# Four dense tiles from bf16 pieces in a graph kernel's counts pass, and two row buffers between its passes

## The reference

```
L0: x += ssp(segment_sum(h[dst] * filter(edge) * cutoff, src) @ W + b) @ W + b
L1: x += attention over edges, softmax by destination, values h @ W
L2: x += relu( (D_dst^-1/2 * segment_sum((D_src^-1/2 h)[src], dst)) @ W + b )
L3: two convolutions, out = segment_sum((dinv h)[src] * ew, dst) * dinv @ W + b, prelu
```

## Time and profile before

| | |
|---|---|
| timed runs | 5455.49, 5463.11, 6915.47 us, median 5463.11 |
| profiled execution | 5453.59 us, span 5451.4 us |
| mean granted clock of TensorE | 0.83 of full over the span |
| node stage and counts pass | 2950 to 3028, 3028 to 3750 us (clock 0.97) |
| node stage and convolution one | 3750 to 3841, 3841 to 4653 us (clock 0.92) |
| node stage and convolution two | 4653 to 4724, 4724 to 5394 us (clock 0.92) |
| busy in the counts pass | PE 576, DVE 344, ACT 197, POOL 492 of 722 us |

### The profile page before, as it was taken

How to read it: one execution, slowest core, us unless ns; L and a number is a source line. 1 busy time by engine, 2 the same in 40 slices (tenths; PEclk the granted TensorE clock), 3 DMA queues, 4 the chain that set the end, 5 groups by cost and what they waited for, 6 DMA issues and landing times.

```text
span 5451.4 us, 88258 instructions
## 1 busy us (share of the span) xinstructions
PE 4081.7 (75%) x26225; PEld 3597.7 (66%) x26225; DVE 2992.9 (55%) x10670; ACT 1657.1 (30%) x3531; POOL 3668.0 (67%) x3340
## 2 busy tenths in 40 slices
PE   3777766676775488888887578886688888688886
PEld 2655555555664377777777466665577877588886
DVE  3655555555551677777776444445444555444445
ACT  3544444444442343333332322222211111111111
POOL 0788888888885277777773676761677777277773
PEclk7877777777777688888887799998799999799998
DMA  6666666666665222222221211110334343344442
GB/s 203 130 115 118 112 118 114 113 114 115 115 107 103 58 56 56 56 55 54 55 54 24 67 52 50 50 50 21 114 129 139 125 143 125 99 149 157 144 156 89
DMA packets 405518, 531.75 MB, mean 98 GB/s; under 512 B 136752, under 2 KB 321689, under 8 KB 398521
## 3 DMA queue, kind: packets, MB, share of 16 engines
q0 software_dynamic: 199680, 221.72, 22.4%
q1 hardware_dynamic: 205496, 305.85, 17.7%
HBM read 374.16 MB, written 153.13 MB: 97 GB/s over the span
## 4 chain that ended last, share of the span: by engine, by line
PE 40%; issue 16%; DMA 15%; DVE 14%; POOL 9%; DVEq 2%; SPq 1%; ACT 1%; POOLq 0%; ACTq 0%
DMA sums<-G,idx 14%; POOL sums L736 9%; PE psF L1210 8%; PE psC L1210 8%; PE psC L1143 4%; PE psE L1196 4%; PE psD L1196 4%; PE psA L1133 3%; DVE S L1732 3%; PE psB L1185 2%; PE psA L1185 2%; DVE early L1721 1%; DVEq L490 1%; DVE G L1638 1%; PE psD L1148 1%
## 5 line engine op out<-in xcount | busy, mean ns | idle before, releaser
L711 POOL DMA_INDIRECT G<-table,idx x1664 | 1595.5, 959 | 857.0 <-issue 496.1
L736 POOL DMA_INDIRECT sums<-G,idx x832 | 1283.7, 1543 | 370.5 <-issue 200.4
L693 POOL DMA_INDIRECT G<-table,idx x832 | 785.7, 944 | 285.1 <-issue 253.8
L967 ACT COPY arena<-psA 128x600 f32<-128x600 f32 x312 | 206.0, 660 | 1222.9 <-PE psA L1185 1159.0
L1083 PE MATMUL psE<-arena,stage 128*128 128x128 f32 x832 | 211.3, 434 | 441.5 <-ACT G L887 441.3
L1083 PEld LDWEIGHTS psE<-arena,stage 128*128 128x128 f32 x832 | 181.1, 321 | 526.1 <-ACT G L887 526.1
L1210 PE MATMUL psC<-arena,stage 128*128 128x144 f32 (+1 forms) x3822 | 504.4, 291 | 0.0
L1210 PE MATMUL psF<-arena,stage 128*128 128x144 f32 (+1 forms) x3822 | 504.1, 292 | 0.0
L1210 PEld LDWEIGHTS psF<-arena,stage 128*128 128x128 f32 x3822 | 493.1, 201 | 0.0
L1210 PEld LDWEIGHTS psC<-arena,stage 128*128 128x128 f32 x3822 | 492.1, 200 | 0.0
L1494 DVE TENSOR_TENSOR arena<-psB,G 128x1024 f32<-128x1024 f32 x104 | 127.4, 1225 | 648.7 <-PE psB L1064 648.7
(11 more groups left out here) (281 smaller groups left out, 7997.0 us busy)
## 6 DMA issues: line engine op xcount, KB each, us to landing
adjacency<-arena SPq DMA_DIRECT2D x26, 2400.0 KB
arena<-adjacency SPq DMA_DIRECT2D x26, 2400.0 KB
acc<-in_src_row SPq DMA_DIRECT2D x104, 512.0 KB
arena<-in_dst_row SPq DMA_DIRECT2D x104, 512.0 KB
G<-table,idx POOLq DMA_INDIRECT x2496
sums<-G,idx POOLq DMA_INDIRECT x832, 3.4
sums<-arena SPq DMA_DIRECT2D x4, 3300.0 KB, 26.9
table<-stage SPq DMA_DIRECT2D x28, 448.0 KB, 3.0
```

Of the source, the lines that this page charges most:

```text
L693: pool.indirect_dma_start(G[st.r][:, t * width:(t + 1) * width], None, tables[n], bass.IndirectOffsetOnAxis(ap=idx[st.r][:, t:t + 1], axis ...
L711: pool.indirect_dma_start(G[at.r][:, t * D:(t + 1) * D], None, tables[n], bass.IndirectOffsetOnAxis(ap=idx[at.r][:, t:t + 1], axis=0)).the ...
L736: pool.indirect_dma_start(sums_dram[t % SUMS], bass.IndirectOffsetOnAxis(ap=idx[st.r][:, t:t + 1], axis=0), G[st.r][:, t * TW:(t + 1) * TW ...
L967: A.copy(dense_at(at.g, m.loaded + j, k % GROUP), counts_in((k * m.built + j) % 2)).then_inc(mixed["kept"], 1)
```

## The change

In the counts pass four tiles are dense and four thin. Its planes are bf16, which is exact for these counts. The node rows are split into three bf16 pieces, h0 = bf16(h), h1 = bf16(h - h0), h2 = bf16(h - h0 - h1), so that three bf16 products per block replace one fp32 product. ScalarE makes the first piece, VectorE the other two. The rows themselves lie in another place in SBUF (`h_split`), from which the table is written; ScalarE waits for that write before its planes overwrite it.

In the prologue and before pass 3 the rows of a batch go to one of two buffers (`h_turn`), and ScalarE does a batch's rows ahead of the previous batch's copies. Before pass 4 the copy to `stage` goes from VectorE to ScalarE, and VectorE waits for it before it writes the next h7.

```diff
-    for n, what in ((2, (3, 0, False, True)), (3, (2, 0, True, False)), (4, (3, STORED, False, False))):
+    for n, what in ((2, (4, 0, False, True)), (3, (2, 0, True, False)), (4, (3, STORED, False, False))):
...
+        half_planes = 4 * PLANE // 2
+        dense16 = [arena[:, behind + 7 * CHUNK - half_planes:].bitcast(BF16), arena[:, 0:half_planes].bitcast(BF16)]
+        h_split = arena[:, behind + 7 * CHUNK - BLOCKS * D:]
+        h_part = [arena[:, half_planes:half_planes + BLOCKS * D // 2].bitcast(BF16),
+                  stage[:, 0:BLOCKS * D // 2].bitcast(BF16), stage[:, BLOCKS * D // 2:BLOCKS * D].bitcast(BF16)]
+        h_rest = [arena[:, k * BW:(k + 1) * BW] for k in range(2)]
...
+        h_turn = {0: [h7, t7], 3: [h7, u7]}
...
-                        batch_before(act, s["tr"] if n in (0, 3) else s["rows"], j)
-                        if n == 3:
-                            batch_before(act, s["rows"], j)
+                        if j >= 2:
+                            reached(act, s["tr"], j - 1)
+                        if n == 3 and j >= 2:
+                            reached(act, s["rows"], j - 1)
...
-                        to = stage[:, at] if to_stage else h7[:, b * D:(b + 1) * D]
+                        to = h_split[:, at] if to_stage else h_turn[n][j % 2][:, b * D:(b + 1) * D]
...
-            rows_of(0)
-            lhs_of(0)
-            with act.Fori(1, NJ) as j:
-                rows_of(j)
-                table_rows_0(j - 1)
+            for j in range(NJ):
+                if j + 1 < NJ:
+                    rows_of(j + 1)
+                if j > 0:
+                    table_rows_0(j - 1)
                 lhs_of(j)
...
-            batches(act, normalized(2, to_stage=True))
+            rows_of = normalized(2, to_stage=True)
+
+            def first_part(j):
+                reached(act, nd[2]["rows"], j + 1)
+                A.copy(h_part[0][:, batch(j)], h_split[:, batch(j)]).then_inc(nd[2]["h"].sem, 1)
+
+            for j in range(NJ):
+                rows_of(j)
+                if j > 0:
+                    first_part(j - 1)
+            first_part(NJ - 1)
+            act.wait_ge(table_out, 16 * (TABLE_DMAS[1] + NJ))
...
-            batches(act, lambda j: (rows_of(j), acc_of(j)))
+            for j in range(NJ + 1):
+                if j < NJ:
+                    rows_of(j)
+                if j > 0:
+                    acc_of(j - 1)
...
-            skewed(act, lhs_of, acc_of4)
+
+            def acc_and_stage(j):
+                acc_of4(j)
+                reached(act, nd[4]["h"], j + 1)
+                A.copy(stage[:, batch(j)], h7).then_inc(nd[4]["rows"].sem, 1)
+            skewed(act, lhs_of, acc_and_stage)
...
+                    terms = h_part if m.counts else [stage]
                     for h in range(part * BLOCKS // GROUP, (part + 1) * BLOCKS // GROUP):
...
+                        for q, term in enumerate(terms):
+                            ins = M.matmul(segments((psC, psF)[at.g][:, 0:m.dense * SEG], m.dense), term[:, h * D:(h + 1) * D],
+                                           segments(planes(m, at.g)[:, 0:m.dense * PLANE], m.dense)
+                                           [:, :, h * SEG:(h + 1) * SEG],
+                                           start=(h == 0 and q == 0), stop=(h == BLOCKS - 1 and q == len(terms) - 1))
...
-            reached(dve, s2["rows"], NJ)
+            for j in range(NJ):
+                reached(dve, s2["h"], j + 1)
+                link(V.tensor_tensor(h_rest[j % 2], h_split[:, batch(j)], h_part[0][:, batch(j)], ALU.subtract))
+                link(V.tensor_copy(h_part[1][:, batch(j)], h_rest[j % 2]))
+                V.tensor_tensor(h_part[2][:, batch(j)], h_rest[j % 2], h_part[1][:, batch(j)], ALU.subtract)
...
-            batches(dve, rows_to_stage(s3))
+            for j in range(NJ):
+                reached(dve, s3["h"], j + 1)
+                V.tensor_copy(stage[:, batch(j)], h_turn[3][j % 2]).then_inc(s3["rows"].sem, 1)
...
             def node_4(j):
+                batch_before(dve, s4["h"], j)
                 prelu(s4, j, rowb["b0"])
                 batch_before(dve, s4["tr"], j)
+                batch_before(dve, s4["rows"], j)
...
-                rows_to_stage(s4)(j)
```

More of the change, by code:

```diff
@@ L496, in counts_in, with planes, dense_at @@
                 .rearrange("p b (h w) -> p b h w", w=SLOTS)
-        def dense_at(g, t, place):
-            return dense[g][:, t * PLANE:(t + 1) * PLANE]\
+        def planes(m, g):
+            return (dense16 if m.counts else dense)[g]
+        def dense_at(m, g, t, place):
+            return planes(m, g)[:, t * PLANE:(t + 1) * PLANE]\
                 .rearrange("p (b h s) -> p b h s", b=2, s=SEG)[:, :, :, place * SLOTS:(place + 1) * SLOTS]
@@ L549, in one @@
                     sp.dma_start(tables[n][bass.ds(j * BW, BW), :].rearrange("(b p) f -> p b f", p=P),
-                                 tiles(stage[:, batch(j)], BJ)).then_inc(table_out, 16)
+                                 tiles((h_split if n == 2 else stage)[:, batch(j)], BJ)).then_inc(table_out, 16)
                 with sp.Fori(0, NJ) as j:
@@ L1032, in _ @@
             M.matmul(psE[:, 0:P], ones[:, :], tmp[1][:, :], start=True, stop=True).then_inc(pro["rows"], 1)
-            batches(pe, lambda j: (batch_transposes(0, j), batch_products(0, W["in"], j)))
+            for j in range(NJ):
+                batch_transposes(0, j)
+                batch_products(0, W["in"], j)
             pe.wait_ge(pro["flag"], 1)
@@ L1262, in _ @@
             batches(pe, lambda j: batch_products(3, W["gc"], j))
-            batches(pe, lambda j: batch_transposes(3, j))
+            for j in range(NJ):
+                batch_transposes(3, j)
             weighted_pass(3)
@@ L1822, in _ @@
             norm_columns(3, dinv[:, BLOCKS:2 * BLOCKS])
-            def rows_to_stage(s):
-                def body(j):
-                    reached(dve, s["h"], j + 1)
-                    V.tensor_copy(stage[:, batch(j)], h7).then_inc(s["rows"].sem, 1)
-                return body
-            batches(dve, rows_to_stage(s3))
+            for j in range(NJ):
+                reached(dve, s3["h"], j + 1)
+                V.tensor_copy(stage[:, batch(j)], h_turn[3][j % 2]).then_inc(s3["rows"].sem, 1)
             start_pass(3, "resid bn rows turned")
```

12 lines of the change are left out of this document (6 added, 6 removed).

## The result

| | before | changed |
|---|---|---|
| timed runs, median | 5458.36 us (four, 5455.49 to 5463.11) | 5495.94 us (five, 5493.75 to 5496.51) |
| ratio to before | | 1.0068, 95% interval 1.0057 to 1.0080 |
| profiled execution | 5453.59 us, span 5451.4 | 5494.40 us, span 5492.5 |

The change makes the kernel 38 us slower, 31 to 44 by the interval. I had forecast no change (+2 us on the profiled execution, 5462 in the runs). One of before's timed runs, 6915 us, is a disturbed one and is left out.

What follows compares the result with a forecast made beforehand. A counts-pass ring of count, VectorE, gathered and dense products was taken as the bound; 9 + 2.2 + 1 - 13.5 + 3.5 = +2 us gave 5456 profiled, 5462 us timed with 5.7 added; 8-in-10 range 5430 to 5510.

Steps and rivals of the forecast that it cites:

- What bounds the kernel: Counts pass: each chunk is a 6.48 us ring of count, VectorE, gathered and dense products; GpSimd is near the limit.
- VectorE's link, +0.30 us: Counts chunk, count to first gathered product: another one-hot and add cost 0.52 us, one thin one-hot fewer saves 0.22.
- Gathered products -0.24, dense products +0.03: Counts chunk: eight gathered instructions for ten, -0.24 us; three bf16 instructions per block for two fp32, 0.0826 us each, +0.03.
- The two rivals of a floor: Bf16 dense products: 0.1118 us floor per pair, 5577 us, chance 0.07; a quarter of that excess, 5491, chance 0.13.
- Part of it: Rival on bf16 dense products: a quarter of the floor's excess, 0.0893 us each, +29 us, 5491; chance 0.13.
- The clock falls more often: Rival in the counts pass: dense work goes from 3.0 to 4.4 us once per four chunks, +36, 5498; chance 0.08.
- Into the counts pass +1: Node stage before the counts pass: first gather 4.0 us later, first one-hot 8.6, mostly covered; +1 us, bounds -4 and +5.
- Into convolution one -13.5: Stage before convolution one: with two buffers ScalarE makes rows during transposes, batches take 3.5 us, first gather 13.5 us earlier.
- Into convolution two +3.5: Stage before convolution two: the staging copy on ScalarE lengthens a batch ring by 0.80 us; +3.5 us, bounds -4 and +9.
- Prologue 0: Prologue: two buffers gain nothing, since table writes wait for SyncE's zeroing until 87.02 us; cover for 4.7 us of loss.
- my two conditions for being wrong: Counts pass: wrong if the ring is not where VectorE ends it, or if the bf16 stream is off 0.083.
- The sign that failed: Counts pass, one of the listed signs of a right forecast: chunks of 6.55 to 6.6 us.

Runs made afterwards that it cites:

- The kernel with four buffers: The changed kernel with four instead of two pairs of one-hot buffers in the counts pass, order unchanged; 5427.35 us, ratio 0.9937.
- with TensorE full: Changed kernel with four one-hot buffer pairs, thin one-hots after the first pair, adds one pair later, gathered products between second and third count; 5288.17 us.
- the last two kernels: Changed kernel with four one-hot buffer pairs and reordered counts pass, 5288.17 us; the same with the staging copy before convolution two back on VectorE, 5280.96 us.
- the last order: Counts pass on four one-hot buffer pairs: thin one-hots after the first pair, adds one pair later, gathered products between second and third count; 5288.17 us.

## Why the prediction was wrong, point by point

- **What bounds the kernel**: right. The ring of count, VectorE, gathered and dense products set the counts pass, and GpSimd did not. The kernel with four buffers shows it from the other side.
- **VectorE's link, +0.30 us**: this is the step that failed. It is +0.58. I took 0.52 from the earlier trace rows, a place where VectorE had not just waited, so its sequencer had loaded the add's address earlier. Behind a wait the load is in the open, +0.10. And I priced a one-hot by its undisturbed row, while gathers that are in step with the ring stretch the same ones in every chunk, +0.18. Over the pass: the 98 chunks from the sixth on grew by 39.5 us, where 98 x 0.09 = 8.8 was forecast. Chunks longer than 8.1 us hold 8.5 of that (the clock, below). The others grew by 0.32 us on average (0.27 to 0.34 by place in the group) and not by 0.38: 31 us, 22 over the forecast, and all of it VectorE's link, since the gathered and dense products stand in them as forecast. These 22 and 8.5, less 1.3 us by which the first dense chunk, at half clock in before, got shorter, and with 0.3 at the end, make the 29.6 us by which the row of the dense products exceeds its term, within 0.1.
- **Gathered products -0.24, dense products +0.03**: right, at -0.23 and +0.03. The pace of 0.0826 us a bf16 instruction of 192 columns is the one taken; and 144 columns take 0.0626, so there is no floor of 0.1118 under bf16 pairs. That the fp32 load made that floor was not tested. The two rivals of a floor fall; that *Part of it* named 5491, near the 5496 measured, is a coincidence, since its pace of 0.0893 was not there. The estimate of 89 ns from the Trainium skill, TensorE: Matmul & The Clock Gate, section Back-to-back issue gap, is 6 ns too high by this trace, and the measurement decides.
- **The clock falls more often**: this rival was right in kind, at 8.5 us where it priced 36; its 5498 is near the measured time by luck. Eleven chunks of the changed kernel last over 8.1 us, six of before's steady ones. Each of them holds one stretch of 3.4 us in which the granted clock is 0.50, the level of 1.2 GHz, which costs some 1.6 us. Before one of these, from 3173.9 to 3175.9 us, TensorE was busy for 0.93 of the 2 us. It doesn't go with the bits of the counts: with the same counts it is four chunks where the add stands late, three without gathers, and with TensorE full the granted clock is 1.00. All but one are a group's first chunk, in which TensorE waits longest (3.50 us from count to gathered products, before 2.84). But with four buffers, where it waits less in the other chunks, it is still ten, and two without gathers and with the load early, where that wait is 3.46; so what decides is not shown.
- **Into the counts pass +1**: right at +0.7, with one half as worked out and the other 2 us off. The first gather comes 27.35 us after the rows' start instead of 23.07 (+4.3, predicted +4.0), the first one-hot 38.1 instead of 27.5 (+10.6, predicted +8.6), and the first dense product hides both.
- **Into convolution one -13.5**: right to 0.1 us, and all of it stayed.
- **Into convolution two +3.5**: the mechanism was right, the size was not; it is +8.0 in the traces and 7.2 between the last two kernels. The batches pay 4.6 us and not 3: the second and third paid 1.4 and 1.2 where I let them pay 0.6 each, since the granted clock was 0.50 there and the products took 3.35 us where the earlier trace rows has 3.12 and 2.86. The half clock stood in my bounds, not in my term. The other 3.4 us come behind the last of these copies, where my sum left 0.5. From it to the pass's start is 1.1 us more. From that start to the first gather is 5.56 us instead of 1.93: before, VectorE had the last rows in `stage` 2.2 us ahead of the start, and now ScalarE's copy of them ends 0.07 us ahead of it. The wait for indices behind that takes back only 1.3.
- **Prologue 0**: right. ScalarE's last copy is over 2.6 us earlier (79.7 instead of 82.3), and the table write starts at 88.5 us behind the zeroing, before at 87.4.
- **The signs**: TensorE's gap was ended by VectorE and the stream ran at 83 ns, so neither of my two conditions for being wrong came true. The sign that failed was the chunk, 6.86 us where I wrote 6.55 to 6.6.

The fourth tile was a bad trade in this order. Its price stood on the ring that every chunk goes through, and its gain, one gather less, on an engine that in the kernel before nobody waited for. In the last order, where GpSimd is at its limit, that gain counts.

## What to carry to other kernels

When a loop is a ring through several engines, price an added operation at the place in the ring where it stands: right behind a wait, where nothing of it (address loads included) has been done ahead. Before relieving an engine that nobody waits for, ask what breaks the ring; here two more pairs of buffers and another order were worth 208 us, and the gather that the fourth tile saves, worth nothing before, is there what lets the chunk fall to 5.04 us. And when an edit moves an instruction and the total stays, look whether another engine's periodic work ends the wait now.

## What the runs showed of the hardware

- An indirect gather on GpSimd (0.94 us) stretches VectorE's one-hots by up to 0.23 us when they begin about 0.5 to 0.2 us ahead of its end, and not when they have begun earlier; without gathers the stretch is gone.
- A register load on VectorE's sequencer costs 0.10 us behind a semaphore wait (one-hot to one-hot 0.62 us, 0.53 with the load ahead), and nothing where the sequencer runs ahead of the engine (0.52 in the earlier trace rows).
- Pairs of a bf16 weight load and matmul run at 0.0826 us with 192 columns and 0.0626 with 144, which is columns at 2.4 GHz plus 2.6 ns; the weight load's recorded 0.10 us does not show in it.
- A TensorE that waits a little in every chunk was granted 0.97 of its clock over 460 us, one that never waited 1.00.
- GpSimd issues indirect gathers of 128 rows of 512 bytes every 1.25 us, 0.95 busy and 0.30 between them, when nothing holds it up.
